# Expert down projections transposed in fp32r, with gate weights turned by TensorE and spread by DMA, eight steps behind the up projections

## What is computed

```python
scores = jax.nn.softmax(x @ gate_w, axis=-1)
topk_w, topk_idx = jax.lax.top_k(scores, K)                      # K = 2 of E = 8
topk_w = topk_w / (jnp.sum(topk_w, axis=-1, keepdims=True) + 1e-20)
w_per_expert = jnp.einsum('nke,nk->ne', one_hot(topk_idx), topk_w)
for e in range(E):
    hid = jax.nn.silu(x @ w_gate[e]) * (x @ w_up[e])             # 128 -> 256
    y = y + w_per_expert[:, e:e + 1] * (hid @ w_down[e])         # 256 -> 128
shared = jax.nn.silu(x @ ws_gate) * (x @ ws_up) @ ws_down
x = x + y + shared                                               # x normalised before use
```

## Time and profile before

| | before |
|---|---|
| median of 3 runs | 204.2 us (203.9 to 204.35) |
| the profiled execution | 204.34 us, span 202.5 us |
| TensorE busy | 192.2 us, 95% |
| its weight loads | 151.8 us, 75% |
| VectorE busy | 156.7 us, 77% |
| ScalarE busy | 137.2 us, 68% |
| GpSimd busy | 96.5 us, 48% |
| granted TensorE clock | 1.00 |

### The profile page before, as it was taken

How to read it: one execution, slowest core, us unless ns; L and a number is a source line. 1 busy time by engine, 2 the same in 40 slices (tenths; PEclk the granted TensorE clock), 3 DMA queues, 4 the chain that set the end, 5 groups by cost and what they waited for, 6 DMA issues and landing times.

```text
span 202.5 us, 4608 instructions
## 1 busy us (share of the span) xinstructions
PE 192.2 (95%) x1626; PEld 151.8 (75%) x1626; DVE 156.7 (77%) x414; ACT 137.2 (68%) x318; POOL 96.5 (48%) x145
## 2 busy tenths in 40 slices
PE   7999999899999898988999999899989999999995
PEld 7878887677877676755666666576668799999994
DVE  2569998669768885879999999999973876357744
ACT  2399968688668687299989999788977232552220
POOL 7579307778476677607739992003300017500430
DMA  6980405802553015589743300000000000000001
GB/s 170 377 217 6 155 2 191 280 0 50 73 76 43 0 40 123 64 98 109 78 119 88 71 2 3 2 0 3 0 0 3 5 0 0 3 0 13 3 1 38
DMA packets 13301, 12.69 MB, mean 63 GB/s; under 512 B 1072, under 2 KB 11312, under 8 KB 13280
## 3 DMA queue, kind: packets, MB, share of 16 engines
q1 hardware_dynamic: 12176, 11.15, 25.9%
q10 hardware_dynamic: 1008, 1.06, 1.6%
q0 software_dynamic: 96, 0.20, 0.7%
HBM read 10.96 MB, written 1.44 MB: 61 GB/s over the span
## 4 chain that ended last, share of the span: by engine, by line
PE 78%; DVE 11%; ACT 5%; issue 3%; POOL 1%; DVEq 0%; POOLq 0%
PE ps L992 13%; PE ps L951 11%; PE ps L1016 8%; PE ps L877 7%; PE ps L928 6%; PE ps L893 6%; PE ps L761 6%; PE ps L910 5%; PE ps L849 4%; PE ps L733 3%; PE ps L774 3%; DVE low L1212 3%; DVE q_t L1222 3%; ACT q_t L670 2%; ACT prob L636 2%
## 5 line engine op out<-in xcount | busy, mean ns | idle before, releaser
L1222 DVE CUSTOM_DVE_ANT_0 q_t<-ps,mask_add 128x512 f32<-128x512 f32 x64 | 41.4, 684 | 3.4 <-PE ps L910 2.1
L510 POOL TENSOR_TENSOR prob<-prob,rec 128x512 f32<-128x512 f32 x32 | 32.6, 1045 | 21.9 <-DVE rec L1281 21.9
L636 ACT ACTIVATE prob<-ps,low 128x256 f32<-128x256 f32 x64 | 29.5, 484 | 7.0 <-DVE low L1212 7.0
L670 ACT ACTIVATE q_t<-q_t,low 128x512 f32<-128x512 f32 x44 | 29.3, 716 | 3.7 <-DVE low L1222 3.4
L951 PEld LDWEIGHTS ps<-ident,q_t 128*128 128x128 f32 x176 | 19.5, 141 | 8.8 <-ACT q_t L670 2.9
L549 POOL TENSOR_TENSOR place_k<-place_k 128x256 f32<-128x256 f32 x10 | 7.3, 734 | 38.8 <-DVE place_k L1247 38.8
L951 PE MATMUL ps<-ident,q_t 128*128 128x128 f32 x176 | 23.9, 276 | 1.9 <-ACT place_k L714 0.8
L1212 DVE TENSOR_REDUCE low<-ps 128x2 f32<-128x512 f32 x32 | 20.4, 683 | 5.8 <-PE ps L849 5.8
L656 ACT ACTIVATE q_t<-ps 128x512 f32<-128x512 f32 x18 | 10.6, 598 | 21.2 <-PE ps L992 21.1
L1268 DVE TENSOR_TENSOR q_t<-q_t,ps 128x512 f32<-128x512 f32 x18 | 12.2, 684 | 11.4 <-PE ps L992 7.0
L893 PE MATMUL ps<-ident,prob 128*128 128x128 f32 x128 | 17.2, 277 | 2.1 <-DVE prob_t L1285 1.4
(11 more groups left out here) (184 smaller groups left out, 468.5 us busy)
## 6 DMA issues: line engine op xcount, KB each, us to landing
k_stack<-k_dram SPq DMA_DIRECT2D x18, 128.0 KB
wg<-in_L_ffn_w_gate SPq DMA_DIRECT2D x1, 1024.0 KB, 5.7
wu<-in_L_ffn_w_up SPq DMA_DIRECT2D x1, 1024.0 KB, 8.0
q_stack<-q_dram SPq DMA_DIRECT2D x6, 144.0 KB
k_dram<-prob SPq DMA_DIRECT2D x1, 768.0 KB, 3.6
w_in<-in_L_attn_Wq ACTq DMA_DIRECT2D x2, 256.0 KB, 5.7
context<-in_ctx SPq DMA_DIRECT2D x1, 512.0 KB, 6.2
w_in<-in_L_attn_Wv SPq DMA_DIRECT2D x1, 512.0 KB, 8.1
```

The costliest lines, as they stand in the source:

```text
L510: nc.gpsimd.tensor_tensor(pr, pr, rec1[:, s % 2, r, :].unsqueeze(2).to_broadcast([P, C, S]), ALU.mult).then_inc(s_norm1, 1)
L636: e = nc.scalar.activation(prob1[:, s % 3, r, c * S:(c + 1) * S], ps[:, 2 * (s % 2) + r, c * S:(c + 1) * S], ACT.Exp, bias=low1[:, s % 2, ...
L670: nc.scalar.activation(prob2[n % 3][:, c, :], score2[n % 2][:, c, :], ACT.Exp, bias=low2[:, n % 2, c:c + 1], scale=-1.0).then_inc(s_exp2, 1)
L1222: nc.vector.tensor_tensor_reduce(out=score2[n % 2][:, c, :], in0=ps[:, 2 * (n % 2) + c, :], in1=mask_add[:, c, :], scale=1.0, scalar=3e38, ...
```

## The change

- The down projection is transposed and in fp32r: the stationary operand is a part of the down weights, the moving one a part of the hidden tile, and the output is features by 256 tokens, six matmuls of 256 columns (three products for each of the two halves of the hidden features). Both have to be split in high and low parts. GpSimd splits the down weights (`split_down`, in iterations n = 23 to 30, the last in step 4). For the hidden tile VectorE writes the product back into the up projection's PSUM bank, ScalarE copies it as high part (`high_of_hidden`), and VectorE subtracts to get the low part, one step later.
- The up projections rotate over three banks (`U_BANKS`) instead of two; `hid` has nine buffers, and the lag is eight steps.
- The residual is added on TensorE: two fp32 matmuls of `x2` with the identity open the group of the shared expert. In sequence 1 the shared expert comes last.
- With features on partitions, the weight of a token must be spread over all partitions. The chain of gate weights now ends in `w_e`; TensorE turns it (16 rows of 128), ScalarE copies it to SBUF (`turned_w`), a DMA writes it to DRAM and two DMAs read it back, each spread over 128 partitions (`w_wide`).
- Sequence 0: ScalarE copies each down output to SBUF (`raw_output`), GpSimd multiplies it by the spread weights and adds it. Sequence 1: VectorE multiplies, GpSimd adds the first two, VectorE the others; the last output is added in two halves.
- The chain of gate weights is cut in two parts of 8 and 12 operations. For sequence 0 they stand in iteration n = 33 before and after the copy there, for sequence 1 in steps 10 and 11; `turn2`, `gate` and `gate_exp` of sequence 1 are one step later than before.
- The output leaves transposed, in three DMAs, and the host turns it by a view.

```diff
+    N_SELF + 33: [("weights", 0, 0)],
-LAG_D = 2
-BY_POOL = 5
+LAG_D = 8
+HIDS = LAG_D + 1
+U_BANKS = (2, 3, O_BANK)
+BY_POOL = 2
 FFN_BETWEEN = {
-    1: [("weights", 0, 0)],
     3: [("turn_o2", 1, 0), ("turned_o2", 1, 0)],
     4: [("wo2", 1, 0), ("residual2", 1, 0)],
-    6: [("turn2", 1, 0), ("turned2", 1, 0)],
-    7: [("gate", 1, 0)],
-    8: [("shift", 1, 0), ("gate_exp", 1, 0)],
-    11: [("weights", 1, 0)],
+    7: [("turn2", 1, 0), ("turned2", 1, 0)],
+    8: [("gate", 1, 0)],
+    9: [("shift", 1, 0), ("gate_exp", 1, 0)],
+    10: [("weights", 1, 0)],
+    11: [("weights", 1, 1)],
+    2: [("turn_w", 0, PT_BANK), ("turned_w", 0, PT_BANK)],
+    13: [("turn_w", 1, MID_BANK), ("turned_w", 1, MID_BANK)],
 }
+AFTER_COPY = {N_SELF + 33: [("weights", 0, 1)]}
...
+def expert(i):
+
+    b, k = divmod(i, NE + 1)
+    return (k - 1) % (NE + 1) if b == 0 else k
...
+            for b in range(B):
+                sp.wait_ge(s_wrows, b + 1)
+                load(w_dram[b], w_rows, d_wdram)
+                sp.wait_ge(d_wdram, 16 * (b + 1))
+                sp.wait_ge(s_low2, C * N_CROSS)
+                for i in range(2):
+                    rows = slice(i * NE, (i + 1) * NE)
+                    load(w_wide[:, b, i * NE * P:(i + 1) * NE * P],
+                         w_dram[b, rows, :].rearrange("(o r) t -> o (r t)", o=1).to_broadcast([P, NE * P]), d_wwide[b][i])
...
+            for i in range(FFN_EARLY, N_FFN + LAG_D):
+                for kind, row, _ in FFN_BETWEEN.get(i, ()):
                     if kind == "turned2":
                         split_tokens(row)
+                    elif kind == "residual2":
+                        normalise(3 + row, x2, row * C)
+                        split_down(NE)
+                b, k = divmod(i - LAG_D, NE + 1)
+                if (b == 0 and k >= 1) or (b == 1 and 1 <= k <= BY_POOL):
...
+                        link(nc.gpsimd.tensor_tensor(y_tmp, y_part[k % 2], wide_weight(b, expert(i - LAG_D)), ALU.mult))
+                        nc.gpsimd.tensor_tensor(acc[:, b, :], acc[:, b, :], y_tmp, ALU.add).then_inc(s_acc, 1)
...
+            def raw_output(j):
+
+                if j > NE:
+                    return
+                act.wait_ge(s_y, j + 1)
+                if j >= 3:
+                    act.wait_ge(s_acc, j - 2)
+                nc.scalar.copy(acc[:, 0, :] if j == 0 else y_part[j % 2], ps[:, y_bank(j), 0:S]).then_inc(s_yraw, 1)
...
             def silu_step(i):
                 act.wait_ge(s_g, i + 1)
                 if i >= 2:
-                    act.wait_ge(s_hid, i - 1)
+                    act.wait_ge(s_prod, i - 1)
                 nc.scalar.activation(silu[i % 2], ps[:, i % 2, :], ACT.Silu).then_inc(s_silu, 1)
+                if i > LAG_D:
+                    raw_output(i - LAG_D - 1)
+                if i >= 1:
+                    high_of_hidden(i - 1)
                 for what in FFN_BETWEEN.get(i, ()):
                     between(what)
...
-                    if i >= 2:
-                        pe.wait_ge(s_hid, i - 1)
-                    up(2 + i % 2, 1).then_inc(s_u, 1)
+                    if i >= 3:
+                        pe.wait_ge(s_hid, i - 2)
+                    elif U_BANKS[i] == O_BANK:
+                        pe.wait_ge(s_osum, B * NG - 1)
+                    up(U_BANKS[i % 3], 1).then_inc(s_u, 1)
...
+                    if 2 <= j <= NE + 2:
+                        pe.wait_ge(s_yraw, j - 1)
+                    elif j > NE + 2:
+                        pe.wait_ge(s_ypart, j - NE - 2)
+                    if e == NE:
+                        pe.wait_ge(s_x2, b + 1)
+                        for c in range(C):
+                            mm(ps[:, y_bank(j), c * P:(c + 1) * P], x2[:, b * C + c, :], ident[:, :],
+                               start=c == 0, stop=False)
+                    for f in range(FC):
+                        for part, (hi, wi) in enumerate(BIG_PARTS):
+                            last = mm(ps[:, y_bank(j), 0:S], w[:, wi, f, :], hid[j % HIDS][:, hi, f, :],
+                                      start=e != NE and f == 0 and part == 0,
+                                      stop=f == FC - 1 and part == len(BIG_PARTS) - 1)
+                    last.then_inc(s_y, 1)
...
+            def outputs(j):
+
+                b, k = divmod(j, NE + 1)
+                e, y = expert(j), ps[:, y_bank(j), 0:S]
+                if b == 0:
+                    return
+                dve.wait_ge(s_y, j + 1)
...
+                if k == 0:
+                    v.tensor_tensor(acc[:, b, :], y, wide_weight(b, e), ALU.mult).then_inc(s_ypart, 1)
+                    return
+                dve.wait_ge(s_acc, NE + min(k - 2, BY_POOL))
+                v.tensor_tensor(y_part[k % 2], y, wide_weight(b, e), ALU.mult).then_inc(s_ypart, 1)
+                if k > BY_POOL:
...
+                    v.tensor_tensor(acc[:, b, :], acc[:, b, :], y_part[k % 2], ALU.add).then_inc(s_sum, 1)
 
             def hidden_step(i):
                 if i < N_FFN:
+                    bank = ps[:, U_BANKS[i % 3], :]
                     dve.wait_ge(s_silu, i + 1)
                     dve.wait_ge(s_u, i + 1)
...
+                    v.tensor_tensor(bank, silu[i % 2], bank, ALU.mult).then_inc(s_prod, 1)
+                if 1 <= i <= N_FFN:
+                    dve.wait_ge(s_hidhi, i)
+                    to = hid[(i - 1) % HIDS]
+                    v.tensor_tensor(to[:, 1, :, :], ps[:, U_BANKS[(i - 1) % 3], :].rearrange("p (f t) -> p f t", f=FC),
+                                    to[:, 0, :, :].bitcast(F32), ALU.subtract).then_inc(s_hid, 1)
                 if i >= LAG_D:
                     outputs(i - LAG_D)
                 for what in FFN_BETWEEN.get(i, ()):
```

More of the change, by code:

```diff
@@ L121, with y_bank @@
 QSETS = ((0, 4), (4, H2))
-def y_bank(j, c):
-    return O_BANK if j == N_FFN - 1 and c == C - 1 else 4 + j % 2
+def expert(i):
+    b, k = divmod(i, NE + 1)
+    return (k - 1) % (NE + 1) if b == 0 else k
+def y_bank(j):
+    return 4 + j % 2
 def cycle(g):
@@ L331, in build, with wide_weight @@
             "s_g", "s_u", "s_silu", "s_hid", "s_y", "s_ypart", "s_acc"))
-        s_ysum = sem("s_ysum")
-        def chunks(ap):
-            return ap.rearrange("b (c p) d -> p (b c) d", p=P)
+        s_yout, s_sum = map(sem, ("s_yout", "s_sum"))
+        s_prod, s_hidhi, s_wdparts = map(sem, ("s_prod", "s_hidhi", "s_wdparts"))
+        d_wdram = sem("d_wdram")
+        d_wwide = [[sem(f"d_wwide{b}_{i}") for i in range(2)] for b in range(B)]
+        s_wturn, s_wrows, s_yraw = map(sem, ("s_wturn", "s_wrows", "s_yraw"))
+        def wide_weight(b, e):
+            return w_wide[:, b, e * S:(e + 1) * S]
         block = ctx.enter_context(nc.Block())
@@ L392, in _ @@
                     load(wd[:, NE, :, :], a["L0_ffn_ws_down"].rearrange("(f r) n -> r f n", r=P), d_wd)
[L393 to L397, removed]
+            for b in range(B):
[7 more added lines that the diff above has]
+                         w_dram[b, rows, :].rearrange("(o r) t -> o (r t)", o=1).to_broadcast([P, NE * P]), d_wwide[b][i])
+            sp.wait_ge(s_acc, NE)
+            load(out[:, 0, :], acc[:, 0, :], d_out)
+            sp.wait_ge(s_yout, 1)
+            load(out[:, 1, 0:P], y_out[:, 1, 0:P], d_out)
+            sp.wait_ge(d_out, 16 * 3)
         @block.gpsimd
@@ L473, in split_weights, with split_down @@
                 split((wg, wu)[which][:, e, :], [t[:, :] for t in w_parts[which][e]]).then_inc(s_wparts, 1)
+            def split_down(k):
+                if k == 0:
+                    pool.wait_ge(d_wd, 32)
+                    pool.wait_ge(s_score2, C * H2)
+                elif k == NE:
+                    pool.wait_ge(s_pv2, B * NG)
+                split(wd[:, (k - 1) % (NE + 1), :, :], [wd_parts[k][:, i, :, :] for i in range(2)]
+                      ).then_inc(s_wdparts, 1)
             def add_bv2(first, count):
@@ L612, in between @@
             def between(what):
-                kind, b, _ = what
+                kind, b, bank = what
                 if kind == "turned":
@@ L617, in between @@
                     x_hat_evac(3 + b, b)
+                elif kind == "turned_w":
+                    act.wait_ge(s_wturn, b + 1)
+                    if b == 1:
+                        act.wait_ge(d_wdram, 16)
+                    nc.scalar.copy(w_rows, ps[0:C * NE, bank, S:S + P]).then_inc(s_wrows, 1)
                 elif kind == "turned_o2":
@@ L720, in _ @@
                 silu_step(i)
-            out_c = chunks(out)
-            for b in range(B):
-                c = b * C + C - 1
-                act.wait_ge(s_ysum, C * (b + 1) * (NE - BY_POOL))
-                act.dma_start(out_c[:, c, :], y_out[:, c, :]).then_inc(d_out, 16)
+            high_of_hidden(N_FFN - 1)
+            act.wait_ge(s_yout, 2)
+            act.dma_start(out[:, 1, P:S], y_out[:, 1, P:S]).then_inc(d_out, 16)
         @block.tensor
@@ L832, in between @@
                     gate(b)
```

(12 more changed lines are left out.)

130 lines of the change are left out of this document (64 added, 66 removed).

## The result

| | before | after |
|---|---|---|
| median | 204.27 us (203.9 to 204.46, 6 runs) | 208.34 us (208.1 to 208.98, 6 runs) |
| ratio | | 1.021 (95% interval 1.019 to 1.0231) |
| the profiled execution | 204.34 us, span 202.5 | 208.10 us, span 206.1 |

What follows compares the result with a forecast made beforehand. TensorE's instructions were taken to bound the expert stage. 204.2 us, less 1.8 of TensorE work, plus 4.9 of new stalls, gave 207.3; 1.2 for GpSimd collisions made 208.5 us, range 203.9 to 211.3.

Steps and rivals of the forecast that it cites:

- walk: Expert stage's queues followed one operation at a time with traced durations; its new stalls sum to 4.9 us without collisions.
- step 4, low part: Early expert steps without down projections: TensorE's step 4 projection waits for VectorE's low part, 0.2 us.
- step 7, normalised tokens: TensorE has done step 7 at 168.9 us and waits for GpSimd's normalised tokens, 0.7 us.
- down projection 3: It waits for raw output 1, which ScalarE's step 9 exponential and table load delay: 0.6 us.
- up 13, turn of the weights, up 14: TensorE waits for VectorE's low part 10, batch 1's gate weights in step 13, and low part 11: 0.6, 1.1, 0.5 us.
- tail: projection 11, then VectorE's pace: After the last up step: projection 11 waits 0.7 us for its bank; VectorE's 0.80 against 0.71 us costs 0.5 more.
- The collision price: GpSimd blocking two-SBUF-input operations of batch 1's gate chain on VectorE: 0 to 3.5 us, a third taken, 1.2.
- Rival (b): Lag and three banks keep TensorE the bound through step 13: 202.4 us, or 203.6 with a tail stall; chance 0.14.
- (c): The gate chain costs nothing, but the early steps and the tail do: 204.5 us; chance 0.10.
- Rival (d): GpSimd fully blocks the eleven two-input operations of batch 1's gate chain: 210.8 us; chance 0.19.
- (f): A down projection still takes 0.89 us, so 3.2 us more, 211.7; chance 0.04.
- (e): The spread weights return late from DRAM for multiply 9; 2 us later gives 209.3 us; chance 0.09.

Runs made afterwards that it cites:

- kernel with small operands: After, with GpSimd multiplying and adding only 8 of 256 columns of sequence 0's outputs: 206.64 us, ratio 1.0107 to before.
- kernel with the power: After, with GpSimd computing sequence 1's gate exponential as a power of e, so ScalarE's two table loads there go: 209.29 us, ratio 1.023 to before.
- kernel with fills: After, with GpSimd filling an unused 128x512 tile twice in place of multiplying and adding sequence 0's outputs: 207.04 us, ratio 1.0128 to before.
- kernel without the chain: After, with 19 of the 20 gate weight operations of sequence 1 left out: 204.94 us, ratio 1.0033 to before.
- chain in PSUM: After, with five tiles of sequence 1's gate chain in PSUM, so no two-input operation has both inputs in SBUF: 207.4 us, ratio 1.0158 to before.

## Why the prediction held, point by point

TensorE's losses in us, from start to start of matmuls as explained above, against the walk's:

| | walk | measured |
|---|---|---|
| step 4, low part | 0.2 | 0 |
| step 7, normalised tokens | 0.7 | 0.9 |
| down projection 3 | 0.6 | 0.5 |
| up 13, turn of the weights, up 14 | 0.6 + 1.1 + 0.5, and 1.2 for collisions | 1.0 + 1.8 + 0.5 |
| tail: projection 11, then VectorE's pace | 0.7 + 0.5 | 0.6 + 0.9 |
| sum | 6.1 | 6.2 |

From the stage's start to TensorE's last end it took 46.95 us before and 51.06 after, 4.11 more. With 6.2 of losses, TensorE's own work is 2.1 us less, by difference; the prediction had 3.2 less for the down projections, 0.9 more for the residual and 0.2 for the turns, which is 2.1. The rows of the end show the two prices, six matmuls at 0.73 and the residual's four records at 0.48 in this chain (0.71 and 0.45 forecast):

```profile
202.31 0.48 PE ps L1112 x4
202.79 0.73 PE ps L1116 x6
203.54 0.29 DVE place_k L1346
```

The two final additions cost 0.1 us more than before's single operation, not 0.3: VectorE's last end lies 0.39 behind TensorE's before and 0.52 after. The stage as a whole grew by 4.24 us, where the sum said 4.3.

The mechanism was the forecast one; that the total came out within 0.2 us is in part luck, since terms were off and cancelled. Counted in the same way, the waits at up 13, the turn and up 14 are 0.4 + 0.9 + 0.5 = 1.8 us in the kernel with small operands, so without collisions, where the walk had 2.2; the collisions then add 1.5, where it had 1.2. The 0.2 of step 4 never came, and step 7, down projection 3 and the tail are off by 0.2, 0.1 and 0.3.

- **VectorE's queue** is the step that carried the prediction. Its times, less the 0.7 us by which after's stage starts earlier: silu 10 done at 178.0, measured 178.16; low part 10 at 182.5, measured 183.06; weights at 185.0, measured 186.41. The walk without collisions was thus 0.56 us early at low part 10 and 1.41 at the weights. The collisions are 0.61 us ahead of low part 10 and 1.61 in all, so apart from them it was right to 0.2 us.
- **The collision price**, 1.2 taken between 0 and 3.5, measured 1.6. The size was near, the count behind its upper end was wrong. I had let each of eleven operations wait out a GpSimd operation. But a held operation ends as GpSimd's does, and so the next one starts in the 0.08 us between two GpSimd operations (the row at 180.94, 0.17 us, between GpSimd's end at 180.87 and its start at 180.95). At most one operation of the chain is held per GpSimd operation, and five were. Of the other six, two started between two GpSimd operations (180.94 and 184.80), three ran while GpSimd was idle (183.61, 183.82, 186.24), and the one at 179.94, which had begun 0.12 us before a GpSimd operation ended, took its usual 0.18. The kernel with the power is a second case, in which GpSimd did not pause until the chain's last four operations: it ran eight, one of them beside the two large passes, and seven operations of the chain were held, 2.0 us in all. The rule of the Trainium skill (SBUF — State Buffer, Who interferes with whom) that whoever comes first keeps the port for its whole instruction is borne out by all five ends, and also by the fills, which it exempts because they only write; that this rule means 3.5 us here, as I wrote, is not. It means 1.6.
- **Rival (b)** fell at the point named for it: low part 10 and the weights were late for step 13. The kernel without the chain is what it would have looked like, 204.94 us, and even that is not below before, for the early steps and the tail remained. That was the case (c), 204.5; its sum left out the wait of down projection 3, 0.5 us measured, and with it comes to 205.0.
- **Rival (d)** is out by the count above, **(f)** by the 0.72 us per down projection. **(e)** is out too. SyncE's rows of sequence 1's weights:

```profile
187.81 0.32 SPq L370 DMA_DIRECT2D w_dram<-q_rest  x1
189.19 0.80 SPq L370 DMA_DIRECT2D w_wide<-w_dram  x2
```

The spread loads took 4.2 and 5.1 us from issue to landing, so the second was there at 189.6 + 5.1 = 194.7, and multiply 9 started at 196.40 behind VectorE's own low part: a margin of 1.7 us where the walk had 0.1 to 2.7.
- **The tail** was sized 0.3 us too small, 1.5 for 1.2. The pace is right: 0.79 us from one down projection to the next (200.57, 201.36, 202.15). The walk counted five of them at 0.1; it missed that VectorE's first addition waits 0.36 us for GpSimd's last one, at 199.66, with the next multiply, and so TensorE's bank, behind it. Taking that product from GpSimd gave 0.47 back.

What stays open: whether earlier table loads would have helped in after itself, since the one kernel meant to tell replaced them by a slower operation; and what moving the chain forward gives while its tiles stay in SBUF.

## What to carry to other kernels

Before you move work to an engine with "time to spare", walk its queue operation by operation through the step where the moved work meets a chain of small dependent ones, and ask which buffer of the bounding engine each item holds; here VectorE was busy for 80% of the span and yet stopped TensorE for 3.3 us. A dependent chain is free where its own engine would be idle anyway (here VectorE's 2.3 us, while ScalarE loads tables) and expensive a step later. A longer lag hides the result, but takes the filler away from the steps that it leaves, and it does not add banks.

## What the runs showed of the hardware

- A VectorE operation with both inputs in SBUF that starts while GpSimd reads ends 0.02 to 0.04 us after GpSimd's instruction. A one-input tensor_scalar of 128x2 was held as well: 0.68 us beside a GpSimd tensor_tensor (chain in PSUM), and 0.26 beside a GpSimd fill (kernel with fills), where 0.17 is usual. The same section of the Trainium skill (SBUF — State Buffer) lists tensor_scalar among the operations that can take the port pair shared with GpSimd; these two rows agree.
- The first fp32r matmul after a wait takes 0.22 us to the next one instead of 0.118 (183.12 to 183.34 in after), and the same at 187.67: a wait costs TensorE 0.1 us more than itself. The first one behind fp32 matmuls shows it too, without any wait: 172.38 to 172.58 in after, and 188.45 to 188.65 in before, 0.20 each.
- GpSimd's power function took 2.93 us on 128x16, and 0.72 on 128x2.
- In one profiled execution the granted clock fell after TensorE had stood still for 1.90 us. The kernel with the power shows it (columns as in the earlier trace rows); before the fall TensorE had been busy for 0.78 of 2 us:

```profile
186.00:188.00 2.00, 0.78 (x7) 0.79 (x7) 1.86 (x7) 0.20 (x1) 0.31 (x1) 1.00 0.00 0
188.00:190.00 2.00, 1.80 (x9) 1.59 (x9) 1.55 (x3) 1.75 (x5) 0.59 (x1) 0.54 0.02 4
190.00:192.00 2.00, 2.00 (x13) 2.00 (x12) 1.29 (x2) 0.00 (x0) 0.86 (x2) 0.61 0.36 133
```

A mean of 0.54 is near the lower level of 1.2 GHz (0.50). Fp32r matmuls start 0.21 us apart there (189.44, 189.65, 189.86) instead of 0.118, and 9 and 13 records stand in 2 us where 5 us of unbroken work hold 43 to 45. With seven steps of lag in after, the three runs at a mean of 0.992 took 1.7 us more on average than the three at 1.000. After's profiled execution waited 1.67 us at the same place and kept 1.00. So, as far as one trace tells, a stall of TensorE can cost more than its own length. That this is why the runs of after with seven steps of lag scatter is not shown: none of the three slower ones has a trace, and three runs of before, which has no such stall in this stage, also had a mean of 0.992 (205.22, 205.00 and 204.94 us).
